# Cumulative sums of dt by two wide fp32 products per block in place of eight narrow ones

## The reference, cut to what matters

```python
zxbcdt = u @ in_proj_w.T                       # u: layer norm of x
dt = softplus(zxbcdt[..., -NHEADS:] + dt_bias) # 16 heads
xBC = silu(conv4(xBC) + conv_b)                # depthwise, 4 taps
dA = exp(dt * A)                               # A = -exp(A_log)
# for every token t, in order:
state = state * dA_t + (dt_t * x_t) outer B_t
y_t = state . C_t
y = (y + D * xs) * silu(z)
y = y * rsqrt(mean(y * y) + EPS) * gamma
return x + y @ out_proj_w.T
```

## Time and profile before

| what | value |
|---|---|
| median of three runs | 3551.24 us (3545.0 to 3558.86) |
| the profiled execution: span, first to last instruction | 3539.0 us |
| the profiled execution's own time | not listed apart from its span |
| PE busy | 3336.7 us, 94% of the span |
| DVE, ACT, POOL busy | 2723.3, 2574.7, 1810.1 us |
| granted TensorE clock, mean | 0.978 of 2.4 GHz |

### The profile page before, as it was taken

How to read it: one execution, slowest core, us unless ns; L and a number is a source line. 1 busy time by engine, 2 the same in 40 slices (tenths; PEclk the granted TensorE clock), 3 DMA queues, 4 the chain that set the end, 5 groups by cost and what they waited for, 6 DMA issues and landing times.

```text
span 3539.0 us, 64210 instructions
## 1 busy us (share of the span) xinstructions
PE 3336.7 (94%) x24314; PEld 1934.5 (55%) x24314; DVE 2723.3 (77%) x4854; ACT 2574.7 (73%) x4690; POOL 1810.1 (51%) x1355
## 2 busy tenths in 40 slices
PE   6899999999999999999868999999999999999998
PEld 4455555555555555555434555555555555555554
DVE  6798878887779787889977677777777777777764
ACT  6888888888888888887637566677666766666664
POOL 1333333333333342333547887876665765566665
PEclk9899999999999999999878999999999999999999
DMA  5355544365544355445468576777776776767664
GB/s 164 93 117 117 122 96 104 100 126 117 123 100 107 93 123 115 125 99 87 84 121 174 97 129 110 134 147 147 126 136 119 152 134 121 120 129 133 120 113 67
DMA packets 809428, 419.43 MB, mean 119 GB/s; under 512 B 566583, under 2 KB 733879, under 8 KB 807072
## 3 DMA queue, kind: packets, MB, share of 16 engines
q1 hardware_dynamic: 752800, 312.58, 43.4%
q0 software_dynamic: 56320, 102.75, 16.0%
HBM read 176.00 MB, written 101.71 MB: 78 GB/s over the span
## 4 chain that ended last, share of the span: by engine, by line
PE 74%; DVE 7%; DMA 7%; ACT 4%; POOL 3%; issue 3%; SPq 1%; ACTq 0%; DVEq 0%; POOLq 0%
PE pair L1314 9%; PE pair L1362 8%; PE pair L1236 8%; PE pair L1471 8%; PE pair L1284 7%; PE pair L1324 5%; PE pair L1378 4%; PE pair L1393 4%; DMA yT<-yhl 3%; PE pair L1439 3%; PE pair L1440 3%; PE pair L1304 2%; PE pair L1409 2%; PE pair L1295 2%; PE pair L1457 1%
## 5 line engine op out<-in xcount | busy, mean ns | idle before, releaser
L1619 DVE SCALAR_TENSOR_TENSOR cv<-raw,taps,cv 128x512 f32<-128x512 f32 x480 | 429.3, 909 | 42.9 <-ACT cv L2013 38.2
L1864 DVE TENSOR_REDUCE smx<-pair 128x2 f32<-128x514 f32 x512 | 349.3, 685 | 66.3 <-PE pair L1409 66.1
L1236 PE MATMUL pair<-xhT,whi 128*128 128x512 f16 x1280 | 382.5, 381 | 2.7 <-DVE state L1674 1.0
L2284 POOL TENSOR_TENSOR ph<-pf,ph 128x1024 f16<-128x1024 f32 x128 | 291.9, 2281 | 180.1 <-ACT ph L2149 179.6
L1314 PE MATMUL pair<-ohi,yT 128*128 128x512 f16 x1024 | 325.0, 390 | 30.6 <-DMA yT<-yhl 30.6
L2143 ACT ACTIVATE pf<-pair 128x1024 f32<-128x1024 f32 x256 | 261.8, 1023 | 106.6 <-PE pair L1440 94.1
L1284 PE MATMUL pair<-zhi,xhT 128*128 128x512 f16 x1024 | 326.3, 380 | 1.8 <-ACT zs L2055 1.2
L2043 ACT ACTIVATE de<-de,cum 128x128 f32<-128x128 f32 x1024 | 308.4, 388 | 0.3
L2289 POOL TENSOR_TENSOR ohl<-of,ohl 128x256 f16<-128x256 f32 x256 | 216.5, 851 | 110.7 <-ACT ohl L2156 109.2
L2149 ACT CAST ph<-pf 128x1024 f16<-128x1024 f32 x256 | 267.0, 1043 | 4.6 <-PE pair L1459 0.2
L2257 POOL DMA_INDIRECT gat<-rows,slot_i x192 | 195.7, 1019 | 108.3 <-DVE slot_i L1812 74.4
(11 more groups left out here) (267 smaller groups left out, 9969.2 us busy)
## 6 DMA issues: line engine op xcount, KB each, us to landing
de<-cum SPq DMA_DIRECT2D x64, 1024.0 KB, 9.4
rows<-rowt SPq DMA_DIRECT2D x16, 1040.0 KB, 6.5
xin<-x SPq DMA_DIRECT2D x16, 1024.0 KB, 8.9
y<-xin SPq DMA_DIRECT2D x16, 1024.0 KB, 5.2
y<-ob POOLq DMA_DIRECT2D x64, 256.0 KB, 6.3
qb<-qa SPq DMA_DIRECT2D x32, 512.0 KB, 4.4
rbc<-rank SPq DMA_DIRECT2D x63, 256.0 KB, 4.1
wst<-wkv SPq DMA_DIRECT2D x32, 256.0 KB, 4.0
```

The costliest lines, as they stand in the source:

```text
L1236: ins = pe.matmul(bk[:], w[:, k, ws], xt[:, ha, k, :], start=n == 0, stop=n == 3 * KD - 1)
L1619: ve.scalar_tensor_tensor(c_[:], r_[:, t:t + BLK], taps[:, ct, t:t + 1], c_[:], ALU.mult, ALU.add).then_inc(done, 1)
L1864: ve.tensor_reduce(smx[:, qt, 2 * h2:2 * h2 + 2], sc[:, :, 0:NK + 1], AX.X, ALU.max)
L2284: po.tensor_tensor(p_[:, 1], f[:], p_[:, 0], ALU.subtract).then_inc(S.plp, 1)
```

## The change

The four chunks' dt * A lie side by side in `dts[:, 0, :]` as 64 columns. Each group of four fp32 products becomes one over all 64: `upper` by 64 moving columns, and 64 stationary columns by `upper`. The second result is now 64 x 128 (chunk and head on partitions, the chunk's tokens in the free dimension) instead of 16 x 512. The copy cumT, the tile in DRAM and `bc_in` follow: the sums of a chunk are one piece of 8 KB in DRAM where they were 16 pieces of 512 bytes, 2 KB apart. cumT keeps its bytes per partition. In the planner the assumed durations of `cum` (1.9 to 0.6) and `cum_exp` (0.9 to 0.6) change.

```diff
--- before.py
+++ after.py
@@ -481,7 +481,7 @@
         elif name == "logits":
             add("PE", 1.33, step, [("turn", a, c) for c in range(CK)] + [("slice_low", 0)], [("single", [("logits_out", a)])])
         elif name == "cum":
-            add("PE", 1.9, step, [("dt", a)], [("single", [("cum_copy", a)]), ("single", [("cum_exp", a)])])
+            add("PE", 0.6, step, [("dt", a)], [("single", [("cum_copy", a)]), ("single", [("cum_exp", a)])])
         elif name == "conv":
             add("PE", 2.6, step, [("turn", a, CK - 1), ("slice_low", PIECE_OF[b])], [("single", [("raw", a, b)])])
         elif name == "gram":
@@ -542,7 +542,7 @@
         add("DVE", 4.4, ("dt", i), [("dt_exp", i)] + [last(("xdt", CK * (i - 2) + CK - 1))])
         add("SP", 0.5, ("rows_out", i), [("dt", i), ("row_low", i, CK - 1)], extra=11.5)
         add("DVE", 0.3, ("cum_copy", i), [("cum", i)] + [last(("decay", CK * (i - 2) + CK - 1))])
-        add("ACT", 0.9, ("cum_exp", i), [("cum_copy", i)] + [last(("y_in", CK * (i - 2) + CK - 1)), last(("cum_store", i - 1))])
+        add("ACT", 0.6, ("cum_exp", i), [("cum_copy", i)] + [last(("y_in", CK * (i - 2) + CK - 1)), last(("cum_store", i - 1))])
         add("SP", 0.5, ("cum_store", i), [("cum_exp", i)], extra=2.2)
         for k, ct in enumerate(CONVS):
             before = conv_of(i, k - 2) if k > 1 else conv_of(i - 1, NCT - 2 + k) if i else None
@@ -758,7 +758,7 @@
         yield 1.33
         yield Pause(15.0)
         yield ("cum", i)
-        yield 1.9
+        yield 0.6
 
     def convolutions(i):
         for ct in CONVS:
@@ -951,7 +951,7 @@
             return nc.dram_tensor(name, shape, dt, kind="Internal").ap()
 
         rows_d = scratch("rows", (T, ROW), F32)
-        cum_d = scratch("cum", (NBLK, NH, BLK), F32)
+        cum_d = scratch("cum", (NBLK, CK * NH, P), F32)
         rank_d = scratch("rank", (NR, L), F16)
         table_d = [scratch(f"scores{g}", (T, 1), F32) for g in range(G)]
 
@@ -1001,7 +1001,7 @@
             dt_t = sb2(mam, "dt", [P, CK, NH], F32)
             cum_t = sb2(mam, "cum", [P, CK, NH], F32)
             ecum = sb2(mam, "ecum", [P, CK, NH], F32)
-            cumT = sb(mam, "cumT", [NH, BLK], F32)
+            cumT = sb(mam, "cumT", [CK * NH, BLK], F32)[:, 0:P]
             raw = sb2(mam, "raw", [P, BLK + TAPS - 1], F32)
             halo = sb(mam, "halo", [P, NCT, TAPS - 1], F32)
             cv = sb2(mam, "cv", [P, BLK], F32)
@@ -1238,18 +1238,12 @@
                 ins.then_inc(S.conv_mm, 1)
 
             def cum(i):
-                xr = dts[:, 0, :].rearrange("p (c h) -> p c h", c=CK)
+                xr = dts[:, 0, :]
                 q.wait_ge(S.da, i + 1)
                 wait_given_back(q, "cum", i)
-                bk = bank("cum", i)
-                for c in range(CK):
-                    ins = pe.matmul(bk[:, c * NH:(c + 1) * NH], upper, xr[:, c, :], start=True, stop=True)
-                ins.then_inc(S.cum_mm, 1)
+                pe.matmul(bank("cum", i)[:, 0:CK * NH], upper, xr, start=True, stop=True).then_inc(S.cum_mm, 1)
                 wait_given_back(q, "cum", i, n=1)
-                bk = bank("cum", i, n=1)
-                for c in range(CK):
-                    ins = pe.matmul(bk[0:NH, c * P:(c + 1) * P], xr[:, c, :], upper, start=True, stop=True)
-                ins.then_inc(S.cumT_mm, 1)
+                pe.matmul(bank("cum", i, n=1)[0:CK * NH, 0:P], xr, upper, start=True, stop=True).then_inc(S.cumT_mm, 1)
 
             def open_(ch):
                 i, c = divmod(ch, CK)
@@ -2018,7 +2012,7 @@
                 ac.activation(ecum[i % 2][:], cum_t[i % 2][:], ACT.Exp).then_inc(S.ec, 1)
                 q.wait_ge(S.cumT_mm, i + 1)
                 q.wait_ge(S.cum_out, 16 * i)
-                ac.copy(cumT[:], bank("cum", i, n=1)[0:NH, :]).then_inc(S.cumT, 1)
+                ac.copy(cumT, bank("cum", i, n=1)[0:CK * NH, 0:P]).then_inc(S.cumT, 1)
 
             def dec(ch):
                 d_ = decs[ch % 2]
@@ -2349,13 +2343,13 @@
 
             def cum_store(i):
                 q.wait_ge(S.cumT, i + 1)
-                sp.dma_start(cum_d[i], cumT[:]).then_inc(S.cum_out, 16)
+                sp.dma_start(cum_d[i], cumT).then_inc(S.cum_out, 16)
 
             def bc_in(ch):
                 i, c = divmod(ch, CK)
                 q.wait_ge(S.w_mm, ch - 1)
                 q.wait_ge(S.cum_out, 16 * (i + 1))
-                sp.dma_start(de[ch % 2][:], cum_d[i][:, c * P:(c + 1) * P].partition_broadcast(P)).then_inc(S.bc[ch % 2], 16)
+                sp.dma_start(de[ch % 2][:].rearrange("p h t -> p (h t)"), cum_d[i][c * NH:(c + 1) * NH, :].rearrange("h t -> (h t)").partition_broadcast(P)).then_inc(S.bc[ch % 2], 16)
 
             def mamba_done():
                 q.wait_ge(S.o, NCH)
```

## The result

| | median us | runs | ratio to before |
|---|---|---|---|
| before | 3549.95 | 4 | 1 |
| changed | 3523.02 (3521.51 to 3533.72) | 4 | 0.9932, 95% interval 0.991 to 0.9955 |

Set against before twice more on other chips, the changed kernel gave 0.9909 (0.9877 to 0.994) and 0.9944 (0.9923 to 0.9966). The forecast was 16 us less, 3535 us. The profiled execution of the changed kernel took 3533.72 us with a span of 3532.4: the slowest of its four, so the two spans (3539.0 before) understate the difference.

A forecast was written before the change was run, and what follows sets the result against it. PE was taken to bound the kernel from 200 to 1600 us. Wide products -19.7 and the fill +3.5, other terms 0, gave -16.2 us: 3551.2 to 3535.0 us, with an 8-in-10 range of 3520 to 3555.

The forecast's parts named there:

- rival B: Fill costs nothing and `gate` gains 4 us from the short `bc_in`: -25, so 3526 us; chance 0.21.
- PE sets the pace from 200 to 1600 us: PE busy 98.7% of that stretch, so time on PE is time of the kernel; ACT, DVE and DMAs have room.
- The price of the wide products: On PE: two wide products take 0.465 us for 1.88, saving 1.41 us a block, 19.7 us over 14 blocks.
- The one piece in DRAM: `bc_in` in 8 KB pieces could give back 0 to 12.1 us of PE's yT waits; taken as 0.
- The fill in the new order: Ahead of 200 us: block 0's last silu and `open` about 7 us later, net 3.5 us lost, bounds -1 and 9.5.
- The new order: the rest: From 200 to 1600 us, PE waits gained or lost by the new order: 0, bounds -8 and +8.
- The end: DVE-bound stretch from 1600 to 1800 us keeps its work, start moves with PE's: 0, bounds -4 and +4.
- The table loads: Eight more on ACT at 1.283 us, 10.3 us, hidden in ACT's idle time at no cost; bound 10.3 us.
- Rival E: The wide product on PE costs by columns: -7, so 3544 us; chance 0.05.
- Rival D: Slower: ACT's order holds up `open` in about five blocks, 7 us each: +19, so 3570 us; chance 0.10.
- What lies outside the span: Median of the runs is 12.2 us above the profiled span, including difference between runs; the change touches neither.
- The attention part: Behind 1800 us: keeps its sequence on PE and ACT; a shift of nothing.

The follow-up runs named there:

- the wide old order: The changed kernel with the planner's assumed durations of before (cum 1.9, cum_exp 0.9): 3498.64 us, 0.9889 of before; repeats 0.9885 and 0.9933.
- fourfold run: The changed kernel with the planner's durations of before and each of the two wide products issued four times: 0.9935 of before.

## Why the prediction was right, and where it was right by luck

The forecast of 16 us less was on the right side and short by 8, because terms of the sum were off in both directions. By the mark (single executions, or means of three) the way from before to the changed kernel is -15.6 for the wide products, -9.6 for the one piece and +3.0 for the new order, -22.2 in all; the forecast had -19.7, 0 and +3.5. That the three misses left 8 us is luck, and the time came out at the number of rival B (3526) rather than at its own.

- PE sets the pace from 200 to 1600 us: right. Products taken out of it moved the end of the Mamba part with everything else held still (15.6 us; 1.21 us a block of the 1.26), and products put back moved it the other way (9 to 13 us). Where bc_in is short the price is not one for one: of 20 us put back 10.6 showed. The distance of 102.9 us between blocks is a mean with the first, of 73.0 us, in it; from the sums of block 1 on it is 105.0 before and 103.1 in the changed kernel, which does not change the sum.
- The price of the wide products: 0.62 us a block where 0.465 was forecast, so 1.26 us saved and not 1.41; over 14 blocks 17.6 us and not 19.7. The per-product price taken from long runs is right as a slope, (1.95 - 0.62) / 6 = 0.22 us, but the two standing alone take 0.155 us more than the 0.465 put down for them. In time the wide products are worth 24 us with pieces; the interval of that is 14 to 34 us, so it does not contradict 17.6.
- The one piece in DRAM: this is the step that was mis-sized. "I take 0" stands in the prediction, and it measured 19 us in the old order (0.9947), by the mark 13.5 us. The reasoning looked at who waits for bc_in, and nobody does. What counts is who is issued behind it. The prediction had the row that shows this, the issue of 8.67 us, and called it an effect of up to 12.1 us, but it counted only the waits between 200 and 1600 us. With the narrow products the largest single part was the one in the fill, 6.5 us, with the fall of the clock behind it. With the wide ones the one piece is worth 9.6 us by the mark in the old order and some 33 in the new one, and the wait in the fill stays in the old order (3.69 us); there its gain is not placed.
- The fill in the new order: the mechanism was right and the size off. The silu came 10.4 us later and not 7, beyond the bound of 9.5; the 1.48 us of idle on ACT that the prediction took off became two waits of 0.91 us. At the first proj PE stands 8.55 us later than before, with one `z` more done (13 records, 2.8 us): 5.7 us lost, but with the gain of the wide products in it. With products and pieces held still (the wide old order, first proj at 141.32) it is 10.9 - 2.8 = 8 us, and the table above has 8 us too: 3.5 was forecast.
- "The new order: the rest" at 0 with bounds of 8: with the sums in pieces it is far outside the bounds (27 us in all, some 20 of it behind the fill); in the changed kernel the full stretch is at 0, as forecast. The end, put at 0 with bounds of 4, gains 6 us, outside its bounds, and with that cancels most of the fill. No run shows why the end got shorter. The same order, with the same wide products, ends the Mamba part 33 us later when a transfer that no step waits for is long.
- The table loads: eight more, 1.283 us each. Two of them stand ahead of the late silu (four loads from 88 to 117 us in place of two) and are 2.6 of its 10.4 us. Behind the fill they did no harm that any run shows; ACT is busy 86.8% from 200 to 1600 us.
- Rival E (price by columns) is refuted: eight wide products in a row take 1.95 us, eight narrow ones 1.88. The Trainium skill, page "TensorE: Matmul & The Clock Gate", section "Wait — 56ns, not 53.3ns?", sets the distance of two matmuls by the moving columns, with a floor of about 25 ns; these fp32 products, at 0.11 to 0.13 us a record from 16 to 128 columns, don't follow it. The prediction also drew the rule too simply. With the floor in it, an estimate by the page is 4 x 25 = 100 ns for four matmuls over 16 columns and 64 / 2.4 + 2.5 = 29 ns for one over 64, so the page too speaks for the wide product.
- Of rival B the mechanism was true (yT waits of 3.5 us in place of 12.1) and its premise, a fill that costs nothing, false. Rival D did not happen: open waited long in block 0 only, and behind 200 us once for xsT, 1.0 us.
- What lies outside the span is 1.3 us (3533.72 and 3532.4 in one execution); the rest of the 12.2 us that the prediction carried along is difference between executions.
- The attention part was left at nothing. Its single executions differ by up to 35 us with the same sequence on PE, so a few us there can be neither shown nor excluded.

## What to carry to other kernels

A transfer that nobody waits for can still have a price: it can delay the transfers issued behind it. Look in the DMA issuer's timeline for long issues behind it, and at whether an engine that is otherwise full waits for those. When an order is computed from assumed durations, a change of them is a change of its own: run the new work in the old order and the old work in the new order, and the two parts come out separately. Correcting an assumed duration towards the true one is no reason for the order to get better: here it went from 1.9 (true 1.88) to 0.6 (true 0.62), and the order cost up to 27 us.

## What the runs showed of the hardware that was not expected

- fp32 products cost nearly the same with 16, 64 and 128 moving columns: 0.112 us a record at 16, 0.110 and 0.116 (fourfold run) at 64, 0.11 to 0.13 at 128, two records a product. Narrow ones waste the difference. At 512 columns it ends: a record of `state` takes 1.71 / 4 = 0.43 us, in the trace of the narrow products with one piece in the new order:

```profile
1426.55 1.88 PE L1304 MATMUL pair<-xw,btok 128*128 128x512 f32 x4
1428.26 1.04 PE L1261 MATMUL pair<-cst,xsT 128*128 128x128 f32 x8
```

- A broadcast of 1 MB from DRAM lands in 9.4 us when its source is cut into 512 byte pieces and in 4.9 us in pieces of 8 KB, while the share of the DMA engines over the full stretch only falls from 0.51 to 0.45.
- Long waits of PE are followed by a lower clock, which costs nearly as much again: after the 3.6 us wait at 143.6, 0.86 from 145 to 160 us, and 1.00 there in the kernel that did not wait. After 2.09 us of waiting at 827.26, also before, it is 0.64 from 827.2 to 832. Not every such wait has it: the fourfold run waits up to 2.4 us at a time and has 1.00 in every window of 15 us from 150 to 1560 us. As a mean of the two levels, 0.86 over 15 us is some 4 us at 1.2 GHz (2 x 0.14 x 15) and the rest at 2.4 GHz.
